# Attention inside a fused transformer block: new orders on ScalarE and VectorE, masks loaded earlier, and the V product of two units in one run

## The reference, cut to what matters

```python
scores = jnp.einsum('bhqd,bhkd->bhqk', q / math.sqrt(HEAD_DIM), k)
scores = scores + attention_bias                      # 2 x 16 x 2048 x 2048, float32
scores = jnp.where(src_mask, -jnp.inf, scores)        # 2 x 1 x 2048 x 2048, uint8
probs = jax.nn.softmax(scores, axis=-1)
ctx = jnp.einsum('bhqk,bhkd->bhqd', probs, v)
```

## Time and profile before

| | |
|---|---|
| median of three runs | 4273.12 us |
| the profiled execution's own time | 4273.3 us |
| its span, first to last instruction | 4271.5 us |
| attention, first `qk` to the last `parts_sum` | about 625 to 3082 us |
| TensorE busy over the span | 93%, granted clock 0.963 of full speed |
| VectorE, ScalarE, GpSimd busy | 59%, 48%, 46% |

### The profile page before, as it was taken

The page is one execution under the profiler, slowest core; times in us unless marked ns, Lnnn a source line. Parts: engine busy times, 40 slices in busy tenths (PEclk is TensorE's granted clock), DMA queues, the critical chain, the costliest instruction groups (busy, mean ns, idle before and its releaser), DMA issues. The chain is left out here.

```text
span 4271.5 us, 80740 instructions
## 1 busy us (share of the span) xinstructions
PE 3975.1 (93%) x32225; PEld 2567.9 (60%) x32225; DVE 2513.5 (59%) x4544; ACT 2058.8 (48%) x2938; POOL 1949.0 (46%) x787
## 2 busy tenths in 40 slices
PE   4999988999989999989999989999889999999997
PEld 2544546777767777767777667777644444444443
DVE  5767657777767777767777777777621211111202
ACT  1111116777767777757777667777611111111110
POOL 2324217666647666656666656666421111111100
PEclk8999988999989999989999999999999999999996
DMA  3232248888878888878888878888530000000005
GB/s 121 89 118 108 89 182 269 282 285 285 285 235 294 282 281 282 281 253 278 284 283 280 270 254 284 281 279 277 201 125 21 20 21 30 30 22 18 1 11 176
DMA packets 201316, 797.27 MB, mean 187 GB/s; under 512 B 23394, under 2 KB 57314, under 8 KB 125700
## 3 DMA queue, kind: packets, MB, share of 16 engines
q1 hardware_dynamic: 193156, 777.68, 53.8%
q10 hardware_dynamic: 7808, 14.68, 1.0%
HBM read 716.26 MB, written 76.02 MB: 185 GB/s over the span
## 5 line engine op out<-in xcount | busy, mean ns | idle before, releaser
L886 POOL TENSOR_TENSOR at_tiles<-at_tiles,at_negmask 128x1536 f32<-128x1536 f32 x512 | 1596.7, 3138 | 854.7 <-DMA at_tiles<-in_bias 729.0
L966 ACT ACTIVATE at_tiles<-at_tiles,at_rmin 128x2048 f32<-128x2048 f32 x512 | 1025.6, 2003 | 252.2 <-DVE at_rmin L1023 252.0
L920 PE MATMUL at_ps_p<-consts,at_tiles 128*128 128x128 f32 x8192 | 1111.2, 279 | 22.4 <-ACT at_prob_t L974 2.0
L920 PEld LDWEIGHTS at_ps_p<-consts,at_tiles 128*128 128x128 f32 x8192 | 934.3, 143 | 160.1 <-ACT at_prob_t L974 139.6
L974 ACT ACTIVATE at_prob_t<-at_ps_p 128x512 f32<-128x512 f32 x1280 | 754.9, 591 | 103.1 <-PE at_ps_p L920 32.9
L1023 DVE CUSTOM_DVE_ANT_0 at_tiles<-at_ps_s,at_tiles 128x1024 f32<-128x1024 f32 x512 | 626.8, 1224 | 272.6 <-PE at_ps_s L904 269.9
L904 PE MATMUL at_ps_s<-at_k_stack,at_q_stack 128*128 128x512 f32 x2048 | 630.6, 429 | 82.7 <-DVE at_rmin L1023 71.3
L1023 DVE CUSTOM_DVE_ANT_0 at_tiles<-at_ps_s,at_tiles,at_rmin 128x1024 f32<-128x1024 f32 x512 | 654.5, 1278 | 0.9 <-issue 0.8
L1032 DVE COPY at_prob_t<-at_ps_p 128x512 f32<-128x512 f32 x768 | 529.7, 690 | 201.9 <-PE at_ps_p L920 201.4
L937 PE MATMUL at_ps_c<-at_prob_t,at_v 128*32 128x128 f32 x16384 | 554.2, 276 | 33.7 <-DVE at_ctx_rows L1041 5.4
L937 PEld LDWEIGHTS at_ps_c<-at_prob_t,at_v 128*32 128x32 f32 x16384 | 416.9, 110 | 137.9 <-DVE at_ctx_rows L1041 92.7
(11 more groups left out here) (170 smaller groups left out, 3022.3 us busy)
## 6 DMA issues: line engine op xcount, KB each, us to landing
at_tiles<-in_bias SPq DMA_DIRECT2D x512, 1024.0 KB, 6.0
at_k_stack<-k_hi SPq DMA_DIRECT2D x128, 256.0 KB, 6.9
at_k_stack<-k_lo SPq DMA_DIRECT2D x128, 256.0 KB, 8.6
at_q_stack<-q_hi SPq DMA_DIRECT2D x128, 128.0 KB, 7.5
at_q_stack<-q_lo SPq DMA_DIRECT2D x128, 128.0 KB, 8.2
at_v<-v SPq DMA_DIRECT2D x64, 256.0 KB, 9.8
em_x_in<-in_x SPq DMA_DIRECT2D x8, 1024.0 KB, 6.6
x<-em_res SPq DMA_DIRECT2D x8, 1024.0 KB, 8.4
```

Source lines behind the costliest of these rows:

```text
L886: pool.tensor_tensor(tiles[:, s, 0:PCOLS], tiles[:, s, 0:PCOLS], negm[:, s, 0:PCOLS], ALU.add).then_inc(s_pool, 1)
L920: last = pe.transpose(ps_p[k][:, y * P:(y + 1) * P], tiles[:, s, t * P:(t + 1) * P], ident)
L966: act.activation(tiles[:, s, :], tiles[:, s, :], ACT.Exp, bias=rmin[:, s, 1:2], scale=-1.0, accum_out=rsum[:, s:s + 1]).then_inc(s_exp, 1)
```

## The change

On ScalarE the turn becomes: `parts` (even), takes of chunks 0 and 2, `exp(u+2)` in place of `exp(u+1)`, and on an even turn the take of chunk 3. Before the loop stand `exp(0)` and `exp(1)`. On VectorE `take(u, 1)` moves behind the second half of the scores. On TensorE the 64 products of `pv` of a pair stand together in the even turn; the odd turn has none. The masks have four buffers instead of two, and SyncE loads those of the next block (32 loads in all, 24 of them on ScalarE's queue before), two units ahead of the conversion's turn.

```diff
+    MRING = 4
...
+            def load_mask(w):
+                after(sp, s_nm, w - MRING + 1)
+                sp.dma_start(mask8[w % MRING][:], mask_v[w]).then_inc(s_mask[w % MRING], 16)
...
             for n in range(NH):
                 for s in range(RING):
+                    ahead, si, _, _, hi = place(n * RING + s + 2)
+                    if hi == HEADS - 1 and ahead + 1 < NH:
+                        load_mask((ahead // HEADS + 1) * RING + si)
...
-                if 2 <= u < NU + 2:
-                    pv((u - 2) // 2, u % 2)
+                if u % 2 == 0 and 2 <= u < NU + 2:
+                    pv((u - 2) // 2)
...
             exp(0)
+            exp(1)
             for u in range(NU + 7):
-                n, s, b, qh, h = place(u)
                 if u % 2 == 0 and 4 <= u < NU + 4:
                     parts((u - 4) // 2)
-                if u + 1 < NU:
-                    exp(u + 1)
                 if u < NU:
-                    for c in range(CH):
-                        if not dve_takes(u, c):
-                            take(u, c)
-                if u < NU - RING and h == HEADS - 1:
-                    w = (n // HEADS + 1) * RING + s
-                    act.wait_ge(s_nm, w - 1)
-                    act.dma_start(mask8[s % 2][:], mask_v[w]).then_inc(s_mask[s % 2], 16)
+                    take(u, 0)
+                    take(u, 2)
+                if u + 2 < NU:
+                    exp(u + 2)
+                if u < NU and not dve_takes(u, 3):
+                    take(u, 3)
...
                 if u + 2 < NU:
                     scores(u + 2, 0)
-                if u < NU and dve_takes(u, 1):
-                    take(u, 1)
                 if u % 2 == 0 and 4 <= u < NU + 4:
                     context((u - 4) // 2)
                 if u + 2 < NU:
                     scores(u + 2, 1)
+                if u < NU and dve_takes(u, 1):
+                    take(u, 1)
                 if u < NU and dve_takes(u, 3):
                     take(u, 3)
```

More of the change, by code:

```diff
@@ L786, in attention_stage @@
         v_sb = [sb(f"at_v{i}", [P, KT, HD]) for i in range(2)]
-        mask8 = [sb(f"at_mask8_{i}", [P, S], U8) for i in range(2)]
+        mask8 = [sb(f"at_mask8_{i}", [P, S], U8) for i in range(MRING)]
         negm = sb("at_negmask", [P, RING, S], BF16)
@@ L800, in attention_stage @@
         s_bias = [sem(f"at_bias_in{i}") for i in range(RING)]
-        s_mask = [sem(f"at_mask_in{i}") for i in range(2)]
+        s_mask = [sem(f"at_mask_in{i}") for i in range(MRING)]
         s_kin = [sem(f"at_k_in{i}") for i in range(2)]
@@ L863, in _ @@
                 load_bias(u)
[L864 to L868, removed]
+                load_mask(u)
             load_v(0)
@@ L921, in transposes, with pv @@
                     last.then_inc(s_pt[k], 1)
-            def pv(pr, part):
+            def pv(pr):
                 n = pr * 2 // RING
[L926 to L929, removed]
-                    for c in range(CH):
-                        k, i = bank(2 * pr + 1, c)
-                        pe.wait_ge(s_pe[k], i + 1)
-                for i in range(part * QUART // 2, (part + 1) * QUART // 2):
+                after(pe, s_cxo, pr)
+                if pr % 4 == 0:
+                    pe.wait_ge(s_vin[n % 2], 16 * (n // 2 + 1))
+                for c in range(CH):
+                    k, i = bank(2 * pr + 1, c)
+                    pe.wait_ge(s_pe[k], i + 1)
+                for i in range(QUART):
                     for g in range(4):
@@ L938, in pv @@
                                          start=(i == 0), stop=(i == QUART - 1))
-                if part == 1:
-                    last.then_inc(s_pv, 1)
+                last.then_inc(s_pv, 1)
             def parts_sum(pr):
@@ L960, in _ @@
             cxv = net.ctx.rearrange("(b q t p) c -> (b q) p t c", p=P, t=RING, q=QH)
-            mask_v = net.given["mask"].rearrange("b o (t p) k -> (b o t) p k", p=P)
             def exp(u):
@@ L1010, in convert @@
             def convert(w):
-                i = w % 2
-                dve.wait_ge(s_mask[i], 16 * (w // 2 + 1))
+                i = w % MRING
+                dve.wait_ge(s_mask[i], 16 * (w // MRING + 1))
                 v.tensor_scalar(negm[:, w % RING, :], mask8[i][:], MASKED, None, ALU.mult).then_inc(s_nm, 1)
```

## The result

The changed kernel takes 4403.5 us in the median of four runs (4394.60 to 4408.47), the kernel before 4272.13 beside it. The ratio is 1.0305, with a 95% interval of 1.0285 to 1.0326: slower, 3.5 us above the forecast of 4400. The profiled execution took 4394.6 us, the shortest of the four, with a span of 4392.8. TensorE's share of it fell from 93% to 87%.

A forecast was written before the change was run, and what follows sets the result against it. The kernel was taken to be bound by a 9.16 us loop per pair over four engines, replaced by one over `parts` of 9.87. 4273.3 + 182 for the loop - 55 for the borders = 4400 us, range 4325 to 4465.

The forecast's parts named there:

- The old loop of 9.16: Kernel before: a loop over four engines, with `exp` ahead of the take TensorE needs, sets the pair at 9.16 us.
- The new loop over `parts`, 9.87: Changed kernel: seven steps from the odd turn's `qk` through `exp`, `parts` and `pv` sum to 9.87 us; +182 us.
- A stall of 1.3 us per pair in front of `parts_sum`: TensorE needs 8.60 of the pair's 9.87 us, so it waits about 1.3 us for `parts`, about 330 in all.
- the first rival: TensorE becomes the bound because `parts` is not late: pair of 8.60 us, 4075 us in all; chance 0.06.
- The queue of ScalarE at 3.44 against 3.46: Odd turn's `exp`: ScalarE's own queue allows it at about 3.44 us after `qk` starts, the scores at 3.46; nearly tied.
- `pv` in one run saves 0.14: On TensorE, joining the halves of `pv` saves one entry into it, 0.14 us a pair, already in the sum.
- The borders give back 55: Early masks end VectorE's waits; a border costs 8 us instead of 26.4, so three give back 55 (bounds 16 and 79).
- The start and the end at nothing: Start: up to 4 us gained from earlier masks, as much lost to early `exp(1)`, set to nothing; end keeps its order.
- The time: Forecast for the whole kernel: 4273.3 + 182 - 55 = 4400 us.
- the same to 0.03 and slower to 0.89: Chances given to outcomes: same 0.03, and slower 0.89, all of the forecast and the clock; faster had 0.08.
- The borders' rival: Loop is 9.45 us and all 79 us of the borders come back: 4268 us, about the same; chance 0.04.
- The clock rival: Stalls of 1.3 us drop TensorE to 1.2 GHz, 1.7 us per T lost: 4509 us, or 4835 if every pair; chance 0.07.

The follow-up runs named there:

- e4: Kernel before with only the masks changed: four buffers, loaded ahead by SyncE, ScalarE's mask loads taken out; 4223.27 us, ratio 0.9887.
- e3: Kernel before with only `pv` of a pair put in one run in the even turn; 4365.21 us, ratio 1.0220.
- e7: Changed kernel plus a 128x512 copy on ScalarE per pair, in the odd turn ahead of the take of chunk 0; 4401.50 us, ratio 1.0299.
- e6: Changed kernel plus a 128x512 copy on ScalarE per pair, directly ahead of `parts`; 4566.18 us, ratio 1.0689.
- e1: Changed kernel with `parts` moved into the odd turn, ahead of its `exp`, on ScalarE; 4078.21 us, ratio 0.9546.
- e2: Changed kernel with `pv` in two halves again, one in each turn; 4181.33 us, ratio 0.9797.
- e5: Changed kernel with `parts` ahead of the odd turn's `exp` and `pv` in halves, one in each turn; 4118.18 us, ratio 0.9636.
- e10: Changed kernel plus a 128x1024 copy into bf16 on ScalarE per pair, ahead of `parts`; 4758.96 us, ratio 1.1141.
- e9: Changed kernel plus a 128x256 copy on ScalarE per pair, ahead of `parts`; 4483.95 us, ratio 1.0492.

## Why the prediction was right, point by point

**The old loop of 9.16.** Right. e4 leaves the orders alone and its pair stays 9.16. In e3 the same loop, with `pv` whole, gives 9.50.

**The new loop over `parts`, 9.87.** Right: 9.88, with each step within 0.02 of its term. e7 against e6 shows that the same 0.52 us cost a pair 0.52 in this loop and nothing beside it, where they fit into idle time, e1 that the loop goes when `parts` stands one place forward, e2 that `pv` is in it with its whole length.

**A stall of 1.3 us per pair in front of `parts_sum`.** Right as the profile counts it, 1.33 x 247, but two things cancel in it. The mis-sized term is TensorE's own work: 8.60 in the forecast, 8.27 in e1, since the odd turn, whose T is followed by `qk`, takes 3.01 and not 3.20, and `parts_sum` 0.17 and not 0.32. So 1.61 us of the pair are lost. 1.48 of them lie in front of `parts_sum`, which starts 2.75 behind its `qk` (1507.68 to 1510.43) and in e1 1.27; the profile calls 1.32 of it idle, because the modelled end of the product ahead covers the rest. The forecast of the time didn't rest on this term, the first rival's 4075 did. That e1 came to 4078, so near to this rival's number, is luck: 0.33 too much for TensorE's own work stood against a loop of 8.59, with a late chunk worth 0.32, that the forecast didn't have.

**The queue of ScalarE at 3.44 against 3.46.** They do tie: in the pair shown S1 ends at 1508.08, the take ahead of `exp` at 1508.10, and `exp` starts at 1508.12. No run tells apart which of the two holds it.

**`pv` in one run saves 0.14.** Right for the entry alone (0.13 in e5), with 0.19 more for the turn whose T now goes straight into `qk`, which the forecast missed. But that is no account of the edit, whose length in the loop costs 0.87. From before, the early masks give -49 (e4), the new orders with halves -42 (e2 against e4), and `pv` whole in these orders +222 (after against e2): +131 in all. In the old orders `pv` whole costs 93.

**The borders give back 55.** A little low: 61, at 6.5 us a border rather than 8. The mean conversion was the 2.2 of the forecast at the first border, and 2.1 over all three. e4 shows the gain without the rest: 58 us in the trace of an execution that is 60 shorter than the one profiled before, 49 between the medians.

**The start and the end at nothing.** The attention's part accounts for 122.2 of the 121.3 us between the two profiled executions, so nothing is left for them.

**The time.** That it came within 3.5 us is in part luck: the four runs of the changed kernel lie 14 us apart, and between the two profiled executions it was +127 in the forecast and +121 in the traces. In the chances, the forecast added up the same to 0.03 and slower to 0.89; by their own terms these are 0.02 and 0.90.

**The borders' rival.** Out: its loop of 9.45 would have to be 9.88, though 61 of its 79 us did come back.

**The clock rival.** Its price was near, 1.5 us for a fall against 1.7, and its threshold was left open. The forecast placed the stall nearer to 0.6 than to 2.8. With one wait in a pair, the runs show no fall inside a block at 1.32 us, a single one at 1.63, and one in eleven pairs at 1.85. The 2.77 us of the earlier trace rows do not stand alone, as the forecast took them to. After 0.70 us of `qk` comes another wait, of 1.01, and the clock falls inside that one (the stretch from 1247 to 1248 has 0.85 granted, the next 0.50). So that row is no measure of what one wait does:

```profile
1247.85 1.22 PE L904 MATMUL at_ps_s<-at_k_stack,at_q_stack 128*128 128x512 f32 x2 [1.01 <-DVE at_rmin L1023]
```

## What to carry to other kernels

Follow one iteration start to start over in-order queues until a row repeats; the sum of the steps is the period, and an instruction outside that chain is free as long as it fits into idle time there. When a short instruction is moved behind a long one, ask who waits for the short one, and what is queued behind the waiter: here 0.26 us of `parts` behind 2.00 of `exp` cost 325 us in all. Whether to join or split work is decided by the loop that it lies in: joining `pv` cost 0.87 us a pair in one order, 0.34 in another, and saved 0.15 in a third.

## What the runs showed of the hardware

**The clock and regular waits.** With one wait in each pair of 9.9 to 10.8 us, and away from the borders, TensorE stayed at its full clock (granted 1.00, 2.4 GHz) for waits of 1.32 us and, with one exception in 237 pairs, for 1.63. Behind waits of 1.85 it fell to 0.50 (1.2 GHz) in one pair of eleven, and behind 2.28 in one of three, at 1.5 us for each fall. The Trainium skill (TensorE: Matmul & The Clock Gate, "A second HAM failure mode: psum-queue depth-cycling") says that frequent short idles between groups of matmuls made the clock swing in one kernel; e6 and e10 agree, the kernel after and all but one pair of e9 show waits at which it didn't.

**GpSimd and the conversions.** The conversion of 3.92 us at 1889.12 began 0.30 after the start of a GpSimd instruction of 3.13. 2.83 for the rest of that and its own 1.22 are 4.05. The Trainium skill (SBUF — State Buffer, "Who interferes with whom") says that the second one blocks for the whole instruction; this agrees within 0.13. It holds the other way round as well: a GpSimd instruction that began at 2527.87, 0.10 after the start of a conversion of 1.22, took 4.10 us, where others take 3.1. At the borders it is the mean conversion that counts, 2.1 us.
